# Decoder block on one core: the router's logits, the scatter waits and one exponential put in other places

## The chip, the cores and the metric

One core of one Trainium2 chip runs the whole kernel in one launch. The metric is the device time of that launch in microseconds, lower is better. In what follows PE is TensorE, DVE is VectorE, ACT is ScalarE, POOL is GpSimd, SP is SyncE.

## What is computed

A decoder block on x of shape (16, 256, 256): 16 sequences of 256 tokens of width 256, 16 heads of 16. All in float32.

```python
x = _layernorm(x + self_attention(x))       # causal; q and k normalised per head before the scores
x = _layernorm(x + cross_attention(x, ctx)) # rotary q and k, no mask, biases
x = _layernorm(x + moe(x))                  # 8 experts, 2 per token

def moe(x):
    logits = x @ router_w.T                 # (tokens, 8)
    top_logits, top_idx = top_k(logits, 2)
    probs = softmax(top_logits)
    hmid = gelu(x @ w1[e].T + b1[e]); y = hmid @ w2[e].T + b2[e]
    return sum over the two experts of probs * y
```

## The kernel before

**Blocks and quarters.** The attention part is a software pipeline over 32 blocks: n = 0 to 15 is the self attention of sequence n, n = 16 to 31 ("crossed") the cross attention of sequence n - 16. A block has four head groups, and the pipeline advances by quarters: `for q in range(QUARTERS)`, 153 of them, with r = q % 4. Every engine has this loop written out by hand, and calls in each quarter the steps that are due: `block_at(q, AT)` gives the block n for which q = 4n + AT, `group_at(q, AT)` the block and head group for which q - AT is their running number. Scores are at 8 (so they run in q = 8 to 135), exponentials at 13, the weighing of the values at 14. PE makes the scores twice: once (L531 to L538) for the row maxima that DVE takes (L1158), and once transposed (L561) with the maxima laid in, for ACT's exponential (L904); then it weighs the values (L582), and ACT drains that (L915). PE's scores of a quarter also wait for the exponential of the transposed scores of the quarter before, since they share banks.

**What else a quarter holds.** r = 0: first query and key projection (L635, qk0), transposes of the finished rows (L608, drained by ACT at L880 into x2T), the maxima's transpose. r = 1: second projection (L635, qk1), transposes of the queries (L669, qT, drained at L955), and the router's logits (L718, `rate`), four matmuls of x2T with 8 columns. r = 2: the output's transposes (L680, jobs o0 and o1; DVE divides them at L1252 and L1256), the value projection, the keys' transposes. r = 3: transposes of the divided output (L694, drained by ACT at L890 into onT), output projection (L706, wo), DVE's residual (L1268), and for a batch the counting of tokens per expert (L731, L734). For crossed blocks DVE drains qk0 and qk1 itself, in the rotation (L1225 to L1227). The logits belong to blocks 16 to 31, in q = 89 to 149; a second projection stands in the same quarter in the first ten of them (q = 89 to 125).

**The ring.** All these PE jobs but the scores share two PSUM banks. `ring_places()` walks the quarters in PE's order and numbers the jobs; a job's bank is its number modulo 2, and it waits until the job two numbers before has been drained:

```python
def await_room(pe, job):
    if RING[job] >= 2:
        pe.wait_ge(drained_by(job), RING[job] // 2)
```

In an r = 1 quarter of the crossed part the ring's order is pv, qk1, qT, logits, so the logits wait for the drain of qk1, which is DVE's rotation.

**The router.** DVE copies the logits (L1289, `take_logits`), here at the start of the following r = 2 quarter, and for batches of blocks, mostly two (four tiles of 128 tokens), chooses the first expert (`choose_first`, L1297 to L1305) and the second (`choose_second`, L1319 to L1327, with the same steps in `best`). For a batch that ends in block `last` the first choice is in q = 4 last + 28, the second in q = 4 last + 29; for the last three batches both are in q = 4 last + 26. Every step of a choice waits for the one before it. ACT makes one exponential of the difference of the two logits (L1000, `exp_gap`), in r = 3, after waiting for the second choice, and ahead of the drain of onT. DVE uses it in the same quarter (`combine_weights`, L1335 to L1351). One r = 0 quarter after, the places are known (L1380), and POOL scatters the rows, 128 at a time, into `xs_dram` by indirect transfers (L1615), two in each quarter from then on, each pair behind a wait for the scores of quarter q. Batches end in blocks 17, 19, 21, 23, 25, 27, 29, 30 and 31; those up to 25 have their first pair in q = 4 last + 32. POOL also adds the bias to each block's residual input in r = 0, ahead of that quarter's scatters (L1586, `add_bias`, for block n in q = 4n + 16); it needs the rows and the projection of block n - 2.

**After the quarters** the expert stage runs over 71 tiles (L813 to L835 on PE), and then the last normalisation.

Of the kernel before, what the change touches and what calls it, by code (L numbers as in the profile page):

```python
# [50 lines left out]
LOGITS_AT = 25  # L51
# [32 lines left out]
def ring_places():  # L84
# [7 lines left out]
    for q in range(QUARTERS):  # L92
# [8 lines left out]
        if r == 0:  # L101
            place("qk0", block_at(q, QK_AT))
            n = block_at(q, LN_AT)
            place("x2T", n, n is not None and crossed(n))
        elif r == 1:
            place("qk1", block_at(q, QK_AT + 1))
            place("qT", block_at(q, TURN_Q))
            n = block_at(q, LOGITS_AT)
            place("logits", n, n is not None and crossed(n))
        elif r == 2:  # L110
            place("o1", block_at(q, OUT_AT))
            place("v", block_at(q, V_AT))
            place("kT", block_at(q, TURN_K))
        else:
            n = block_at(q, TURN_X1)
            place("x1T", n, n is not None and crossed(n))
            place("wo", block_at(q, PROJECT_AT))
            place("rank", routed_at(q, RANK_AT))
# [6 lines left out]
def decoder_block(nc, x, xT, ctxT, wqk_self, wv_self, wo_self, wq_x, wk_x, wv_x, wo_x, bo_self, bo_x,  # L125
# [4 lines left out]
    with ExitStack() as ctx:  # L130
# [366 lines left out]
        def _(pe):  # L497
# [265 lines left out]
            for q in range(QUARTERS):  # L763
# [14 lines left out]
                if r == 0:  # L778
                    project_qk(block_at(q, QK_AT), 0)
                    turn_x2(block_at(q, LN_AT))  # L780
                elif r == 1:
                    project_qk(block_at(q, QK_AT + 1), 1)
                    turn_qk("qT", block_at(q, TURN_Q), 0)
                    rate(block_at(q, LOGITS_AT))
                elif r == 2:
# [63 lines left out]
        def _(act):  # L849
# [152 lines left out]
            for q in range(QUARTERS):  # L1002
# [6 lines left out]
                elif r == 3:  # L1009
                    seed_roots(block_at(q, CHAIN_AT), block_at(q, ROOT_AT))  # L1010
                    exp_gap(routed_at(q, RANK_AT))
                    drain_onT(block_at(q, PROJECT_AT))
# [12 lines left out]
                else:  # L1025
                    drain_x1T(block_at(q, TURN_X1))

            act.wait_ge(table_ready, 2)
# [45 lines left out]
        def _(dve):  # L1074
# [307 lines left out]
            for q in range(QUARTERS):  # L1382
# [9 lines left out]
                elif r == 1:  # L1392
                    maxima(group_at(q, SCORE_AT), 0)
                    maxima(group_at(q, SCORE_AT), 1)
                    moments_of(block_at(q, MOMENTS_AT))
                    choose_second(routed_at(q, SECOND_AT))
                    rotate(block_at(q, QK_AT + 1), 1)
                elif r == 2:
                    take_logits(block_at(q, LOGITS_AT + 1))
                    maxima(group_at(q, SCORE_AT), 0)  # L1400
# [142 lines left out]
        def _(pool):  # L1543
# [54 lines left out]
            def scatter(q):  # L1598
                for last in BATCHES:
# [9 lines left out]
                    ends = nt * TOPK if q == QUARTERS - 1 else min(2 * j + 2, nt * TOPK)  # L1609
                    u = group_at(q, SCORE_AT)  # L1610
                    if u is not None:
# [103 lines left out]
```

## Time and profile before

| | |
|---|---|
| median of 3 runs | 1186.8 us (1186.4 to 1188.1) |
| the profiled execution's own time | 1184.3 us |
| its span | 1182.6 us |
| mean granted clock of TensorE | 0.952 |
| PE busy | 1033.5 us (87%) |
| DVE busy | 720.5 us (61%) |
| ACT busy | 597.2 us (51%) |
| POOL busy | 268.0 us (23%) |

Busy time is the union of an engine's instructions over the span. The timeline gives for each instruction (or run of like ones) its start in microseconds from the span's start, its length, and in brackets how long the engine had stood idle and what released it. `x2` means two instructions in one row; for PE the count is of passes recorded. "issue" as a releaser means that the profile shows none close to the start. The granted clock is a share of full speed: 1.00 is 2.4 GHz, 0.50 is 1.2 GHz.

### The profile page before, as it was taken

To read this page: it belongs to the slowest core of one execution; us is meant where nothing else is said; L and a number is where in the kernel's file an instruction comes from. 1 tells how busy PE (TensorE), PEld (TensorE's weight loads), DVE (VectorE), ACT (ScalarE), POOL (GpSimd) and SP (SyncE) were. 2 spreads that over 40 slices of the span, in tenths; PEclk is the share of its full clock that TensorE was granted. 3 is DMA by queue.
4 is the path that set the end of the run, shared out by engine and by line. 5 is a ranking of instruction groups with operands and counts; after the bars stand their busy time and mean duration, and the time that the engine had idled before them with its cause. 6 is when DMAs were issued, how large, how long until landed. Compare 5 with 4: busy or idle time off the path is not lost.

```text
span 1182.6 us, 29067 instructions
## 1 busy us (share of the span) xinstructions
PE 1033.5 (87%) x10925; PEld 769.5 (65%) x10925; DVE 720.5 (61%) x1584; ACT 597.2 (51%) x1024; POOL 268.0 (23%) x309
## 2 busy tenths in 40 slices
PE   6899999999999999998999999876379999999930
PEld 3556666666666666666666666544269999999930
DVE  4656666666677777676768777763524444444446
ACT  3567767767755666565555555644122222222225
POOL 1053332322233200001212111132512222222210
PEclk9999999999999999999999999998579999999975
DMA  7117446455440001000000100011167766777656
GB/s 286 29 41 252 136 162 199 133 180 182 132 134 20 20 12 46 11 11 30 30 30 30 36 23 30 12 40 39 68 199 216 215 215 215 216 216 213 204 198 250
DMA packets 95078, 139.25 MB, mean 118 GB/s; under 512 B 11264, under 2 KB 68992, under 8 KB 93920
## 3 DMA queue, kind: packets, MB, share of 16 engines
q1 hardware_dynamic: 88320, 114.98, 31.2%
q0 software_dynamic: 6624, 22.42, 4.9%
q8 instruction: 91, 1.49, 0.5%
q14 instruction: 43, 0.35, 0.1%
HBM read 76.56 MB, written 60.29 MB: 116 GB/s over the span
## 4 chain that ended last, share of the span: by engine, by line
PE 80%; issue 6%; DVE 6%; ACT 4%; DMA 3%; SPq 1%; another core or an unknown queue 0%; ACTq 0%; DVEq 0%; POOLq 0%
PE PS L824 11%; PE PS L561 11%; PE PS L835 10%; PE PS L582 10%; PE PS L531 5%; PE PS L639 5%; PE PS L635 5%; PE PS L706 4%; PE PS L653 4%; PE PS L680 3%; PE PS L538 2%; PE PS L669 2%; ACT pT L904 2%; PE PS L534 2%; DVE part L1158 1%
## 5 line engine op out<-in xcount | busy, mean ns | idle before, releaser
L1158 DVE TENSOR_REDUCE part<-PS 128x6 f32<-128x768 f32 (+1 forms) x256 | 269.9, 1087 | 126.9 <-PE PS L538 84.8
L904 ACT ACTIVATE pT<-PS 128x768 f32<-128x768 f32 (+1 forms) x256 | 220.9, 915 | 94.1 <-PE PS L561 92.1
L561 PE MATMUL PS<-big 32*128 32x256 f32 (+1 forms) x2048 | 133.5, 373 | 21.3 <-issue 13.7
L1595 POOL TENSOR_SCALAR_AFFINE_SELECT pT<-pT 128x512 f32<-128x512 f32 x128 | 84.5, 661 | 279.0 <-ACT pT L904 275.4
L824 PEld LDWEIGHTS PS<-oT,big 128*128 128x128 f32 x1136 | 139.5, 194 | 5.4 <-ACT oT L1034 1.8
L824 PE MATMUL PS<-oT,big 128*128 128x128 f32 x1136 | 140.2, 277 | 1.0 <-ACT oT L1034 1.0
L561 PEld LDWEIGHTS PS<-big 32*128 32x128 f32 x2048 | 96.2, 185 | 64.3 <-issue 62.9
L582 PE MATMUL PS<-pT,vaug 128*32 128x256 f32 (+1 forms) x2048 | 126.3, 364 | 10.4 <-DVE carry L1365 2.3
L835 PE MATMUL PS<-w2s,qkn 128*128 x568 | 134.5, 380 | 0.2 <-issue 0.2
L1034 ACT ACTIVATE oT<-PS 128x256 f32<-128x256 f32 x71 | 27.3, 384 | 191.9 <-PE PS L813 191.9
L915 ACT ACTIVATE oT<-PS 128x256 f32<-128x256 f32 x128 | 49.1, 384 | 143.9 <-PE PS L582 125.0
L1615 POOL DMA_INDIRECT xs_dram<-rows_all,posi x64 | 62.2, 972 | 251.1 <-DVE posi L1380 185.3
L1636 POOL DMA_INDIRECT p_dram<-pT,rowid x71 | 68.9, 970 | 210.7 <-DVE rowid L1489 206.5
L835 PEld LDWEIGHTS PS<-w2s,qkn 128*128 128x128 f32 x568 | 102.4, 190 | 11.7 <-issue 0.7
L582 PEld LDWEIGHTS PS<-pT,vaug 128*32 128x32 f32 x2048 | 58.8, 110 | 62.5 <-issue 38.0
L1473 DVE TENSOR_TENSOR qkn<-PS,b1T 128x512 f32<-128x512 f32 x71 | 49.1, 692 | 60.8 <-PE PS L824 60.8
L1483 DVE TENSOR_TENSOR pT<-PS,w_self 128x256 f32<-128x256 f32 x71 | 30.1, 425 | 88.7 <-PE PS L835 88.7
L531 PE MATMUL PS<-big 32*128 32x256 f32 x1024 | 74.4, 404 | 4.4 <-ACT pT L904 4.4
L639 PE MATMUL PS<-w_self,xin 128*128 128x512 f32 x128 | 66.5, 645 | 2.7 <-DMA xin<-xT 1.4
L531 PEld LDWEIGHTS PS<-big 32*128 32x128 f32 x1024 | 47.1, 185 | 16.7 <-issue 14.3
L1041 ACT ACTIVATE qkn<-qkn 128x512 f32<-128x512 f32 x71 | 44.7, 630 | 19.7 <-DVE qkn L1473 18.8
L1586 POOL TENSOR_TENSOR xb<-rows_all,bo 128x512 f32<-128x512 f32 x16 | 20.5, 1280 | 127.8 <-DVE y L1268 125.3
(170 smaller groups left out, 1535.9 us busy)
## 6 DMA issues: line engine op xcount, KB each, us to landing
big<-w SPq DMA_DIRECT2D x71, 512.0 KB
xs_dram<-zrow SPq DMA_DIRECT2D x24, 1496.0 KB, 9.2
oT<-xs_dram SPq DMA_DIRECT2D x71, 136.0 KB
xin<-xT SPq DMA_DIRECT2D x16, 256.0 KB, 2.9
w2s<-w POOLq DMA_DIRECT2D x1, 4096.0 KB, 16.4
xb<-x SPq DMA_DIRECT2D x16, 256.0 KB, 11.2
xin<-ctxT SPq DMA_DIRECT2D x16, 256.0 KB, 2.8
big<-nmaxT SPq DMA_DIRECT2D x128, 4.0 KB
```

The lines of the kernel that those rows point to most:

```text
L531: ins = pe.matmul(o, q, a[r0:r1, 1, g, :], start=True, stop=True)
L561: ins = pe.matmul(o, keys, a[r0:r1, 0, g, q0:T], start=True, stop=True)
L582: ins = pe.matmul(o[PADDED * i:PADDED * (i + 1), q0:T], vaug[:, n % 4, kt, head(g, i), :], pT[:, k % 2, i, kt * T:kt * T + T - q0], start= ...
L635: ins = pe.matmul(o[:, e0:e0 + E], a1[:, c, t * P:(t + 1) * P], w[:, c, :], start=(c == 0), stop=(c == KC - 1))
L639: ins = pe.matmul(o, a[:, c, t * P:(t + 1) * P], w_qk[:, c, :], start=(c == 0), stop=(c == KC - 1))
L824: ins = pe.matmul(moe_bank(1, j % 2)[:, f * P:(f + 1) * P], w1s[:, j % W1_BUFFERS, c, f * P:(f + 1) * P], xsT[:, j % 2, c * P:(c + 1) * P] ...
L835: ins = pe.matmul(moe_bank(3, j % 2)[:, 0:E], hact[:, j % 2, c * P:(c + 1) * P], w, start=(c == 0), stop=(c == FC - 1))
L904: act.activation(pT[:, k % 2, 2 * half:2 * half + 2, 0:wide], src, ACT.Exp).then_inc((exp_a, exp_b)[half], 1)
L1158: dve.tensor_reduce(dst, src, AX.X, ALU.max, negate=True).then_inc((max_a, max_b)[half], 1)
L1595: pool.affine_select(d, d, [[0, 2], [0, 2], [1, P]], ALU.is_ge, 0.0, base=0, channel_multiplier=-1).then_inc(masked, 1)
L1615: pool.indirect_dma_start(out=xs_dram, out_offset=bass.IndirectOffsetOnAxis(ap=posi[:, batch_index(last), c:c + 1], axis=0), in_=rows_all[ ...
L1636: pool.indirect_dma_start(out=p_dram, out_offset=bass.IndirectOffsetOnAxis(ap=rowid[:, o, 0:1], axis=0), in_=ye[:, o], in_offset=None).the ...
```

## The change

Three things. The logits (`rate`) go to the front of the other r = 1 jobs on PE, in the ring and in the code, and DVE's copy of them goes ahead of the rotation in the same quarter. POOL's pairs of scatters wait for the scores of quarter q + 1 instead of q. ACT's `exp_gap` goes from ahead of the drain of onT to the end of the r = 3 quarter.

```diff
@@ ring_places
         elif r == 1:
+            n = block_at(q, LOGITS_AT)
+            place("logits", n, n is not None and crossed(n))
             place("qk1", block_at(q, QK_AT + 1))
             place("qT", block_at(q, TURN_Q))
-            n = block_at(q, LOGITS_AT)
-            place("logits", n, n is not None and crossed(n))
@@ TensorE
                 elif r == 1:
+                    rate(block_at(q, LOGITS_AT))
                     project_qk(block_at(q, QK_AT + 1), 1)
                     turn_qk("qT", block_at(q, TURN_Q), 0)
-                    rate(block_at(q, LOGITS_AT))
@@ ScalarE
                     seed_roots(block_at(q, CHAIN_AT), block_at(q, ROOT_AT))
-                    exp_gap(routed_at(q, RANK_AT))
                     drain_onT(block_at(q, PROJECT_AT))
...
                 else:
                     drain_x1T(block_at(q, TURN_X1))
+                    exp_gap(routed_at(q, RANK_AT))
@@ VectorE
                     choose_second(routed_at(q, SECOND_AT))
+                    take_logits(block_at(q, LOGITS_AT))
                     rotate(block_at(q, QK_AT + 1), 1)
                 elif r == 2:
-                    take_logits(block_at(q, LOGITS_AT + 1))
                     maxima(group_at(q, SCORE_AT), 0)
@@ GpSimd, scatter(q)
-                    u = group_at(q, SCORE_AT)
+                    u = group_at(q + 1, SCORE_AT)
                     if u is not None:
                         pool.wait_ge(scores_pe, NG * u[0] + u[1] + 1)
```

On PE, in the r = 1 quarter of a crossed block with a second projection (L582 weighing, L561 transposed scores, L635 projection, L669 queries turned, L718 logits, then L531 and L680 of the next quarter); a piece of the difference, the same in all ten:

```order
 L582 MATMUL PS<-pT,vaug 32x256 x8
 L561 MATMUL PS<-big 128x256 x8
-L635 MATMUL PS<-wx_q,x1T 128x256 x2
-L635 MATMUL PS<-wx_k,xin 128x256 x2
-L669 MATMUL PS<-ident,qkn 128x128 x4
 L718 MATMUL PS<-rw,x2T 128x8 x4
+L635 MATMUL PS<-wx_q,x1T 128x256 x2
+L635 MATMUL PS<-wx_k,xin 128x256 x2
+L669 MATMUL PS<-ident,qkn 128x128 x4
 L531 MATMUL PS<-big 128x256 x8
 L680 MATMUL PS<-ident,oT 128x128 x4
```

The logits went from the last place of the quarter to the one behind the transposed scores; nothing else moved on PE.

On ACT, in q = 143 and after, where the last block's output is drained (L890) and batch 29 has its exponential (L1000). Before:

```order
L982 ACTIVATE chain<-vv,eps 128x2
L984 ACTIVATE chain<-chain 128x2
L1000 ACTIVATE odds<-odds 128x4
L890 ACTIVATE onT<-PS 128x512
L991 ACTIVATE rows_all<-y,shift,chain 128x256 x2
```

And now:

```order
L982 ACTIVATE chain<-vv,eps 128x2
L984 ACTIVATE chain<-chain 128x2
L890 ACTIVATE onT<-PS 128x512
L1000 ACTIVATE odds<-odds 128x4
L991 ACTIVATE rows_all<-y,shift,chain 128x256 x2
```

The drain and the exponential changed places; the normalising of the rows stays behind both.

On POOL nothing changes its place, only the number that the waits on `scores_pe` name. In the changed kernel, from the last pair of batch 17 to the first of batch 19 (L1586 is the addition of the bias):

```order
L1615 DMA xs_dram<-rows_all,posi 34816x272 [waits scores_pe]
L1615 DMA xs_dram<-rows_all,posi 34816x272
L1586 TENSOR_TENSOR xb<-rows_all,bo 128x512 [waits ring_drained_0,row_ready] x2
L1615 DMA xs_dram<-rows_all,posi 34816x272 [waits scores_pe,place_ready,cw_ready]
L1615 DMA xs_dram<-rows_all,posi 34816x272
```

Two additions (blocks 22 and 23) stand directly behind the last pair, as they do before the change.

## Rows read from the trace of the kernel before

**Rows 1.** Page, parts 1 and 4: engine's busy time; the chain that ended last
```profile
PE 1033.5 (87%) x10925; PEld 769.5 (65%) x10925; DVE 720.5 (61%) x1584; ACT 597.2 (51%) x1024; POOL 268.0 (23%) x309
...
PE 80%; issue 6%; DVE 6%; ACT 4%; DMA 3%; SPq 1%; another core or an unknown queue 0%; ACTq 0%; DVEq 0%; POOLq 0%
```

**Rows 2.** Waits of PE, 470 to 780 us: total, times, longest
```profile
PE PS L718 <- DVE sq L1227: 14.1, 10, 1.8
```

**Rows 3.** Timeline, q = 105: start, length, engine, line, operation [idle before]
```profile
580.93 0.60 ACT L880 ACTIVATE x2T<-PS 128x512 f32<-128x512 f32 x1 [0.40 <-PE PS L608]
...
586.27 0.60 PE L669 MATMUL PS<-ident,qkn 128*128 128x128 f32 x4
...
587.11 0.16 DVE L1327 TENSOR_TENSOR odds<-top 128x4 f32<-128x4 f32 x1
...
588.68 1.03 PE L718 MATMUL PS<-rw,x2T 128*128 128x8 f32 x8 [1.81 <-DVE sq L1227]
```

**Rows 4.** Windows (core busy PE, PEld, DVE, ACT, POOL; clock; DMA), then timeline
```profile
478.00:481.30 3.30, 3.30 (x28) 1.97 (x32) 1.46 (x3) 0.00 (x0) 0.00 (x0) 0.50 0.03 7
...
676.00:679.30 3.30, 3.30 (x28) 1.52 (x28) 2.90 (x4) 0.07 (x1) 1.92 (x2) 0.50 0.14 47
...
589.64 1.19 PE L531 MATMUL PS<-big 32*128 32x256 f32 x16
...
597.65 1.15 PE L531 MATMUL PS<-big 32*128 32x256 f32 x16
...
619.13 1.15 PE L531 MATMUL PS<-big 32*128 32x256 f32 x16
...
625.62 1.15 PE L531 MATMUL PS<-big 32*128 32x256 f32 x16
```

**Rows 5.** Timeline: transposed scores with and without scatters; a pair's first scatter
```profile
556.08 1.15 PE L561 MATMUL PS<-big 32*128 32x256 f32 x16 [0.51 <-issue]
...
583.37 1.15 PE L561 MATMUL PS<-big 32*128 32x256 f32 x16 [0.25 <-issue]
...
627.61 0.97 POOL L1615 DMA_INDIRECT xs_dram<-rows_all,posi  x1 [4.25 <-PE PS L531]
```

**Rows 6.** Timeline, q = 133 and the start of q = 134
```profile
776.44 1.15 PE L561 MATMUL PS<-big 32*128 32x256 f32 x16 [0.77 <-issue]
...
779.69 1.94 ACT L904 ACTIVATE pT<-PS 128x1024 f32<-128x1024 f32 x2 [1.91 <-remote]
...
780.86 1.26 PE L531 MATMUL PS<-big 32*128 32x256 f32 x16 [2.28 <-ACT pT L904]
```

**Rows 7.** Timeline, end of q = 103, q = 104: POOL, VectorE, scores
```profile
571.46 0.97 POOL L1615 DMA_INDIRECT xs_dram<-rows_all,posi  x1 [0.30 <-issue]
...
571.68 0.15 DVE L1177 SCALAR_TENSOR_TENSOR chain<-chain 128x2 f32<-128x2 f32 x1
...
571.87 1.90 DVE L1180 SCALAR_TENSOR_TENSOR chain<-vv,chain 128x2 f32<-128x2 f32 x1
...
572.46 1.28 POOL L1586 TENSOR_TENSOR xb<-rows_all,bo 128x512 f32<-128x512 f32 x1
...
574.85 1.15 PE L531 MATMUL PS<-big 32*128 32x256 f32 x16
...
578.54 0.19 DVE L1299 TENSOR_TENSOR sel<-lg,top 128x32 f32<-128x32 f32 x1
...
580.55 0.69 DVE L1225 TENSOR_TENSOR qkn<-PS,cs 128x512 f32<-128x512 f32 x1 [1.14 <-PE PS L635]
```

**Rows 8.** Timeline, q = 143: last output turn, exponential, drain, residual
```profile
824.21 1.08 PE L694 MATMUL PS<-ident,on 128*128 128x128 f32 x4 [2.25 <-issue]
...
826.82 0.20 ACT L1000 ACTIVATE odds<-odds 128x4 f32<-128x4 f32 x1 [7.63 <-issue]
...
826.93 0.58 ACT L890 ACTIVATE onT<-PS 128x512 f32<-128x512 f32 x1
...
831.38 0.69 DVE L1268 TENSOR_TENSOR y<-PS,xb 128x512 f32<-128x512 f32 x1 [3.94 <-PE PS L706]
```

## Prediction

> **What bounds the kernel now.** The page first: TensorE is busy 87% of the span and the chain that ended last is 80% PE [rows 1]. PE runs its instructions in program order, so in the crossing part of the program every idle stretch of PE is lost time, unless a later wait would have taken it anyway. I then asked who PE waits for between 470 and 780 us [rows 2]: the first line is the router's logits (L718), idle for 14.1 us over 10 quarters until the second rotation of VectorE (L1227) is done. Nothing else comes near.
>
> The timeline of one such quarter (q = 105) shows why [rows 3]. PE works without a gap of note up to the turning of the queries, which ends at 586.87. The logits are next in the ring, two jobs behind the second projection, so they need the bank that the rotation reads. VectorE is still choosing experts until 587.27 and rotates only then; PE stands for 1.81 us. The logits' own data lay ready long before: the copy x2T ended at 581.53. The choice falls into four of the ten quarters; the other six share the rest of the 14.1 us, 1.15 each.
>
> **The change, part by part.**
>
> *Logits first.* On PE the four logits matmuls move ahead of the second projection, on VectorE their copy moves ahead of the rotation. The logits now need only x2T and the bank of x2T, both free. No instruction is added. The wait removed is all of the 14.1 us. What could wait instead: the turning of the queries, two jobs behind the logits, needs the copy (0.17 us) that VectorE does after the choice. That makes 587.27 + 0.2 = 587.5; PE, with 1.03 us of logits put in ahead, is through the projection at about 587.35 (the turning started at 586.27). So 0.15 us in the four quarters with a choice, 0.6 in all. The rotation takes its 1.4 us and ends at about 588.9, while the next scores start at 588.1 and end at 589.25 (1.15 long), and the first output turn wants that bank after them: 0.3 us of margin. The drain of the turned queries ends near 589.6 and is wanted at 589.9. Both margins are thin; as I work it out they hold. Term: -13.5 us.
>
> *Clock.* After three of these waits the granted clock fell to its lower level (1.2 GHz, 0.50 in the window) for 3.4 us; the first and the last of the three stand in [rows 4]. The quarter with the second of them took 8.01 us (589.64 to 597.65) where one at 2.4 GHz took 6.49 (619.13 to 625.62): 1.5 us each. Before each fall PE had stood idle and then run the logits, 8 columns wide. Between -4.6 and 0 (or a little above, if new waits do the same); I take all three as gone, since the nearest rows with such a gap have both parts side by side, and only the logits stay. Term: -4.6 us.
>
> *Transfers.* POOL issues four pairs of row scatters for each batch. The wait is the same instruction in the same place; its value is that of the next quarter's scores. A pair starts 1.99 us after a quarter's scores start (627.61 [rows 5] against 625.62). So the first pair leaves the end of an r = 0 quarter, and the last goes from the r = 3 quarter to the next r = 0 quarter; the other quarters keep a pair at the same point. Three effects.
>  - Without the first pair the maxima of the next quarter start sooner: PE's gap before the transposed scores is 0.51 us there against 0.25 without scatters [rows 5]. Four quarters, 0.2 each: -0.8 us.
>  - At q = 133 four scatters run one behind the other, and the release of the exponential comes 2.1 us behind the end of the matmuls that it needs; PE stands 2.28 us for it at 780.86 [rows 6]. With two scatters I expect about half of it: -1.1 us (bounds -2.3 and 0).
>  - The pair's new place collides. Behind each last pair POOL runs two additions of the bias, which the excerpt of POOL's order shows back to back. The row on L1180 is the warning: this VectorE instruction, with two inputs in SBUF, takes 1.90 us where L1177, its like, took 0.15, and ends with POOL's addition at 573.74; it was held from 0.41 us after the second scatter began [rows 7]. In the r = 3 quarter nobody was waiting. In q = 104 the pair will start at 574.85 + 1.99 = 576.84, the second scatter at 578.11, the hold at 578.52: at 578.54 VectorE starts the choice's first comparison (L1299). That is held until about 580.4. The second addition then takes 1.28 us and holds the next one to about 581.8, and the remaining steps end near 582.4. The rotation, which started at 580.55, comes 1.35 to 1.95 us late; qk0's bank, the maxima and the transposed scores come late by as much, and PE has no slack there. I take 1.65 for q = 104, 112 and 120, and 1.1 for q = 128, where no rotation stands behind the choice: +6.0 us. Bounds: 0 (the choice slips through ahead of the additions) and 4 x 2.4 = +9.6.
>
> The Trainium skill, SBUF — State Buffer, "Who interferes with whom", says that a VectorE instruction with two SBUF inputs and a GpSimd instruction that reads SBUF exclude each other for the whole instruction, and that writing transfer descriptors needs the other interface. It speaks against this change's new place for the additions. Taken to the letter, the hold would begin only with the addition's record, at 579.1; nearly all of the choice would be done, and the sum would be about 6 us lower. The 1.90 us of L1180 began 0.59 us before that record, so I go by the row.
>
> *Exponential.* exp_gap moves from ahead of the drain of onT to the end of ScalarE's r = 3 quarter. In the early batches it takes 0.19 us and nobody waits on either side. At q = 143 it matters: PE had turned the last block's output by 824.21 + 1.08 = 825.29, but ScalarE stood in exp_gap's wait until VectorE's choice was through, ran it at 826.82, and only then drained onT (826.93); the output projection followed and the residual at 831.38 waited 3.94 us for it [rows 8]. Now onT can be drained at 825.35: 1.55 us earlier, and from the residual a single chain (moments, normalising, logits, choice, last scatters) runs to the end of the phase. In this chain exp_gap(30) and (31) have nothing behind them that they held. Bounds 0 and -1.6. Term: -1.55 us.
>
> The expert stage after 860 us and the final normalisation keep order and data: 0.
>
> **Sum:** -13.5 - 4.6 - 0.8 - 1.1 + 6.0 - 1.55 = -15.5 us. The profiled execution took 1184.3 us (span 1182.6), so it would be 1168.8; the median of the runs is 1186.8, 2.5 above it, and I put the forecast on the median: **1171.3 us**.
>
> **The rivals.**
>  - *A, no collision.* The choice's comparisons get in ahead of the additions. For it: L1177, with the same kind of inputs, ran through at 571.68 in 0.15 us while the scatter was being issued. Against it: L1180, 0.2 us later, did not. -15.5 - 6.0 = -21.5: 1165.3 us.
>  - *B, the clock falls as often as before.* The new waits of about 1.7 us in the q = 105 kind of quarter come shortly before the logits, and the clock's lower stretches stay three. For it: seven of ten waits made no fall, so it is partly chance. -15.5 + 4.6: 1175.9 us. The Trainium skill, TensorE: Matmul & The Clock Gate, "HAM oscillation", says that gaps in TensorE's work bring the lower clock and that closing them keeps it up; by that the three stretches go, and the trace agrees only so far as each of them stands right behind a gap.
>  - *C, the wait moves on.* The thin margins of the next quarter (0.3 us for the first output turn and for the drained queries) are not there, because semaphores near scatters come late [rows 6]: with 0.8 us in each of ten quarters PE gets 8 us less. -15.5 + 8: 1179.3 us. For it: in a quarter with a choice VectorE goes from the choice into the copy and the rotation without a pause. Against: six of the ten quarters have no choice, and the rotation follows the projection at once.
>  - *D, slower.* The pair with its two additions occupies POOL for 4.9 us just where VectorE has 1.1 us of slack (idle before L1225) and ScalarE 0.4. If the late release (2.1 us), the hold (1.9) and the second addition (1.3) add up in series instead of overlapping, and a lower clock (1.5) follows each, a batch costs 6.8 us; four cost 27.2 instead of 6.0, and -15.5 + 21.2 = +5.7: 1192.5 us. It decides from 5.4 us a batch, the gains of 21.5 shared by four. Against it: the three run at the same time in the rows, and their overlap is almost whole.
>  - *E, no effect of the logits' move.* If the ring's next wait took all of it, only the smaller terms would be left, within 0.2% of before. That is the measurement's own uncertainty, 2.4 us.
>
> **How the numbers follow.** The forecast 0.42, A 0.20, B 0.16, C 0.13, D 0.04, E 0.05. The range reaches from just below A to most of the way to C: 1164 to 1178.5. By itself the forecast's case has 1168 to 1174 (the collision between 1.35 and 1.95 us, the q = 133 term between its bounds). Faster by over 0.2%: forecast, A, B, C, 0.91. Within 0.2%: E, 0.05. Slower: D, 0.04.
>
> **What would show it.** Right: L718 no longer has a VectorE release in PE's waits; an r = 1 quarter with projection takes about 7.0 us instead of 8.2 to 8.8; few lower-clock stretches between 470 and 780 us; L1180 is short everywhere, while an L1299 or L1301 in q = 104, 112, 120 lasts over 1 us, and the weighing or the transposed scores of the following quarter wait for VectorE; the residual of the last block comes 1.5 us after the choice's end less than before, at about 3 us behind it. Wrong: PE waits of 0.5 us or more before L680 in r = 2 quarters (C); no long L1299 or L1301 (A); a wait of 3 us or more in q = 105 (D).

## The result, and the profile after

| | before | changed |
|---|---|---|
| median, measured side by side | 1187.45 us (1186.4 to 1191.03, 4 runs) | 1169.41 us (1169.01 to 1171.78, 4 runs) |
| ratio | | 0.9847, 95% interval 0.9822 to 0.9872 |
| profiled execution | 1184.3 us | 1169.3 us |
| its span | 1182.6 us | 1167.6 us |
| mean granted clock | 0.952 | 0.956 |

The change is faster by 18.0 us in the medians and by 15.0 us in the spans of the two profiled executions. The forecast was 1171.3 us, from a sum of -15.5 between profiled executions. One run of e8 took 1258.13 us at a granted clock of 0.824, where its others have 0.954 to 0.957; its ratio below leaves that run out, its median doesn't (1163.54 us without it). The page of the changed kernel, parts 1 and 4, against [rows 1]:

```profile
PE 1029.7 (88%) x10925; PEld 767.3 (66%) x10925; DVE 724.1 (62%) x1584; ACT 596.7 (51%) x1024; POOL 267.0 (23%) x309
...
PE 80%; issue 6%; DVE 5%; ACT 3%; DMA 2%; SPq 2%; another core or an unknown queue 0%; ACTq 0%; DVEq 0%; POOLq 0%
```

PE bounds it as before. DVE is the one engine that is busy for longer (3.6 us more). PE's waits between 455 and 770 us (total, times, longest), against [rows 2]:

```profile
PE PS L531 <- ACT pT L904: 5.2, 6, 2.3
PE PS L582 <- DVE sq L1227: 3.5, 3, 1.2
PE PS L561 <- issue: 2.4, 8, 0.4
PE PS L582 <- ACT big L955: 2.3, 5, 0.5
PE PS L582 <- DVE carry L1365: 2.3, 5, 0.9
...
PE PS L669 <- DVE lg L1289: 0.7, 4, 0.2
```

The 14.1 us before the logits are gone. In their place stand four waits of 0.17 us for the copy of the logits (four of 0.15 were forecast), and two that take something back: the weighing waits for the rotation (3.5 us in three quarters), and the scores wait for the exponential (5.2 us; before, the same view has it at 0.9 us). Most of both comes from the quarters to which the last pair of scatters has moved, as q = 104 with the start of q = 105. The timeline of the changed kernel, all engines:

```profile
569.36 0.97 POOL L1615 DMA_INDIRECT xs_dram<-rows_all,posi  x1 [4.34 <-PE PS L531]
...
570.63 0.97 POOL L1615 DMA_INDIRECT xs_dram<-rows_all,posi  x1 [0.31 <-ACT oT L915]
...
571.06 3.12 DVE L1299 TENSOR_TENSOR sel<-lg,top 128x32 f32<-128x32 f32 x1
571.63 2.49 POOL L1586 TENSOR_TENSOR xb<-rows_all,bo 128x512 f32<-128x512 f32 x2
...
572.98 1.94 ACT L904 ACTIVATE pT<-PS 128x1024 f32<-128x1024 f32 x2 [2.64 <-remote]
...
574.14 1.15 PE L531 MATMUL PS<-big 32*128 32x256 f32 x16 [0.73 <-ACT pT L904]
...
576.38 1.07 PE L582 MATMUL PS<-pT,vaug 128*32 128x256 f32 x16 [1.09 <-DVE sq L1227]
```

L1299 normally takes 0.19 us [rows 7]. Here it starts at 571.06, 0.57 us before the record of the two additions, and ends at 574.18, with the end of the second (571.63 + 2.49 = 574.12). PE then waits twice, 0.73 us before the scores for an exponential that started late and 1.09 us before the weighing for the rotation: 1.8 us together. L1299 is held in the same way in q = 112, 120 and 128 (3.13, 3.13 and 3.10 us). In the last of these no rotation follows, and nothing on PE waits for VectorE. There the exponential starts 1.71 us behind the end of its matmuls (734.54, beside the two scatters), PE waits 2.29 us for it, and the clock falls (0.50 from 737.50 to 740.90):

```profile
737.42 2.06 PE L531 MATMUL PS<-big 32*128 32x256 f32 x16 [2.29 <-ACT pT L904]
```

A second new wait stands in q = 136, where batch 25 has its four scatters in a row:

```profile
775.74 0.39 PE L561 MATMUL PS<-big 32*128 32x256 f32 x4
...
778.62 1.94 ACT L904 ACTIVATE pT<-PS 128x1024 f32<-128x1024 f32 x2 [2.60 <-remote]
...
780.70 1.15 PE L561 MATMUL PS<-big 32*128 32x256 f32 x16 [2.42 <-ACT pT L904]
```

The matmuls that the exponential needs ended at 776.13; it started 2.5 us later (a late release, in what follows). q + 1 = 136 has no scores, so the last pair of this batch has no wait any more and runs right behind the pair before it. The wait stood there before too, at 0.99 us. Behind the longer one the clock falls a second time (a granted clock of 0.53 from 781.70 to 785.10). The timeline at q = 143, against [rows 8]:

```profile
811.38 1.09 PE L694 MATMUL PS<-ident,on 128*128 128x128 f32 x4 [2.27 <-DVE on L1256]
...
812.50 0.60 ACT L890 ACTIVATE onT<-PS 128x512 f32<-128x512 f32 x1 [6.18 <-issue]
...
813.15 3.39 PE L706 MATMUL PS<-wx_o,onT 128*128 128x256 f32 x8 [0.69 <-issue]
...
816.58 0.69 DVE L1268 TENSOR_TENSOR y<-PS,xb 128x512 f32<-128x512 f32 x1 [1.99 <-PE PS L706]
```

ScalarE drains onT 0.03 us after PE's end, where it stood 1.6 us before.

Where the 15 us went, by the start of each quarter's scores in the two timelines (changed less before): -0.6 lay before the first quarter that the change touches; the ten r = 1 quarters with a second projection, their new waits taken off, gave -14.5; three quarters behind a fall of the clock (q = 90, 106, 118) -4.3; a new fall of the clock in q = 129 some +1.4; the new place of the last pair +5.7 over four batches; q = 133 and 134 -3.0; q = 136 and after +2.3, of which the longer wait makes 1.4 and the second new fall 0.8; the last block -1.95; all other quarters +0.2. That makes -14.8, and the last block's residual stands at 816.58 against 831.38, 14.8 us earlier. The 18.0 us between the medians are more than these two traces account for.

### The profile page after: what moved, and what is told of

Read it like the earlier page. It is cut to its first block, busy times and chain, and to the rows that moved or that the text cites. A ratio compares the mean times of both kernels' runs of the same rounds, so it can differ in the third digit from the quotient of the medians.

```text
span 1167.6 us, 29067 instructions
## 1 busy us (share of the span) xinstructions
PE 1029.7 (88%) x10925; PEld 767.3 (66%) x10925; DVE 724.1 (62%) x1584; ACT 596.7 (51%) x1024; POOL 267.0 (23%) x309
## 4 chain that ended last, share of the span: by engine, by line
PE 80%; issue 6%; DVE 5%; ACT 3%; DMA 2%; SPq 2%; another core or an unknown queue 0%; ACTq 0%; DVEq 0%; POOLq 0%
PE PS L824 11%; PE PS L561 11%; PE PS L835 11%; PE PS L582 10%; PE PS L531 5%; PE PS L635 5%; PE PS L639 5%; PE PS L706 5%; PE PS L653 4%; PE PS L680 3%; PE PS L538 2%; PE PS L669 2%; PE PS L534 2%; ACT pT L904 2%; PE PS L813 1%
## 5 line engine op out<-in xcount | busy, mean ns | idle before, releaser
L561 PE MATMUL PS<-big 32*128 32x256 f32 (+1 forms) x2048 | 133.2, 373 | 20.4 <-issue 11.7
L561 PEld LDWEIGHTS PS<-big 32*128 32x128 f32 x2048 | 95.9, 184 | 62.5 <-issue 61.2
L582 PE MATMUL PS<-pT,vaug 128*32 128x256 f32 (+1 forms) x2048 | 125.0, 361 | 13.6 <-DVE sq L1227 3.5
L582 PEld LDWEIGHTS PS<-pT,vaug 128*32 128x32 f32 x2048 | 58.8, 109 | 64.7 <-issue 39.5
L531 PE MATMUL PS<-big 32*128 32x256 f32 x1024 | 74.2, 404 | 7.0 <-ACT pT L904 6.8
L531 PEld LDWEIGHTS PS<-big 32*128 32x128 f32 x1024 | 47.4, 186 | 20.8 <-issue 18.9
L1268 DVE TENSOR_TENSOR y<-PS,xb 128x512 f32<-128x512 f32 x32 | 22.1, 692 | 40.9 <-PE PS L706 37.3
```

What stands on the lines that cost most here:

```text
L531: ins = pe.matmul(o, q, a[r0:r1, 1, g, :], start=True, stop=True)
L561: ins = pe.matmul(o, keys, a[r0:r1, 0, g, q0:T], start=True, stop=True)
L582: ins = pe.matmul(o[PADDED * i:PADDED * (i + 1), q0:T], vaug[:, n % 4, kt, head(g, i), :], pT[:, k % 2, i, kt * T:kt * T + T - q0], start= ...
```

## Experiments

They were measured in sets: e1 to e4, e5 to e8, e9 and e10, e11 and e12, each set with the kernel before in it. Between sets the absolute times differ: in the last two the kernel before had a median of 1173 and 1178 us, in the earlier ones of 1187 to 1191. It isn't the chip alone: e1 to e4 (1188.75 us before) and e9 and e10 (1173.32) ran on the chip with the same number. So only ratios, or two kernels of one set, are set against each other. "The change" means the whole of it.

**e1_logits: the logits' move alone.** The hunks of the diff on the ring, on TensorE and on VectorE; scatter waits and exponential as before.

> The first part alone: the logits ahead of the second projection, in the ring, on PE and on DVE; the scatters wait as before and exp_gap stands as before. Theory (each part pays or costs what the comparison of the two traces says): the ten r = 1 quarters of q = 89 to 125 lose 1.15 to 1.8 us each and add 0.17 in the four with a choice, 13.5 us in all; the lower-clock stretches behind them go, 4.4 us; the last pair of scatters stays in the r = 3 quarter, so no L1299 lasts over 1 us and q = 104, 112, 120, 128 are as short as before; q = 133 still has its four scatters in a row and its wait of about 2.3 us. Ratio to before 0.984 to 0.986, about as fast as the whole change or 1 to 3 us faster. Rival (the scatter waits are part of the gain, and without them the late signals behind four scatters in a row now reach PE in q = 101, 109, 117, 125, where the stall on the rotation covered them before): PE waits of 1 us or more before the scores of q = 102, 110, 118, 126, and 4 to 8 us less gain, ratio 0.989 to 0.991.

Measured: 1168.22 us, ratio 0.983 (0.9799 to 0.9861). PE's waits, 455 to 770 us:

```profile
PE PS L531 <- ACT pT L904: 4.8, 5, 2.2
PE PS L561 <- issue: 4.3, 12, 0.7
PE PS L582 <- DVE carry L1365: 2.3, 5, 0.9
PE PS L582 <- ACT big L955: 2.0, 5, 0.5
```

No L718, and no L582 behind L1227. q = 104 takes 5.98 us and q = 105 7.22, against 6.78 and 8.02 in the change. The ten r = 1 quarters are 14.0 us shorter than before (13.5 were forecast), and the windows from 455 to 740 us all show a granted clock of 1.00. The scores of q = 135 start 18.5 us earlier than before (18.1 were in my two terms, logits and clock). The logits' move alone brings all that the change brings; nothing here shows that the other parts together add to it.

**e2_waits: the scatter waits alone.**

```diff
-                    u = group_at(q, SCORE_AT)
+                    u = group_at(q + 1, SCORE_AT)
```

> The second part alone: pairs of scatters wait for the next quarter's scores, everything else as before. Theory: L1299 lasts about 3.1 us in q = 104, 112, 120, 128, and each of these costs PE 1.6 us or more (q = 128 about 2.6), q = 136 with four scatters in a row costs about 2.2; q = 101, 109, 117, 125 give 0.2 each, q = 133 gives 2 to 3. Slower by 3 to 6 us, ratio 1.003 to 1.005. Rival (spreading the scatters pays by itself): faster by 1 us or more, ratio under 0.999.

Measured: 1196.06 us, ratio 1.0045 (1.002 to 1.007), slower by 5.4 us (2.4 to 8.3). PE's waits, 470 to 780 us:

```profile
PE PS L718 <- DVE sq L1227: 13.4, 10, 1.8
PE PS L531 <- ACT pT L904: 4.1, 6, 2.4
PE PS L582 <- DVE sq L1227: 4.1, 3, 1.5
```

The wait of the weighing for the rotation stands here too, 4.1 us in three quarters: it comes from the scatter waits, not from the logits' move. The three terms on transfers made +4.1 us. So this part of the change costs time. The trace shows one thing more. With the same ten waits for L1227 as before, five of the quarters behind them take 8.0 to 8.1 us and not 6.5 (q = 94, 102, 106, 114, 126), where it was three in the trace before; in that of e3 it is four (q = 90, 98, 110, 122). How often such a wait brings the lower clock differs from one execution to the next.

**e3_exp: the exponential alone.**

```diff
-                    exp_gap(routed_at(q, RANK_AT))
                     drain_onT(block_at(q, PROJECT_AT))
...
                     drain_x1T(block_at(q, TURN_X1))
+                    exp_gap(routed_at(q, RANK_AT))
```

> The third part alone: exp_gap behind the drain in r = 3. Theory: the residual of the last block comes 1.5 us earlier behind the choice (before: 4.6 us behind the start of L1327) and nothing else moves; 1.2 to 2 us faster, ratio 0.9984 to 0.9990. Rival (the chain behind the residual waits for something else, the scatters of batch 29 and 30 for one, or the exponential's later place costs combine_weights as much): within 0.5 us of before.

Measured: 1189.54 us, ratio 0.9994 (0.9972 to 1.0017). The time can't tell 1.5 us from nothing. The timeline at the last block can:

```profile
831.42 0.60 ACT L890 ACTIVATE onT<-PS 128x512 f32<-128x512 f32 x1 [6.01 <-issue]
...
832.86 0.21 ACT L1000 ACTIVATE odds<-odds 128x4 f32<-128x4 f32 x1 [0.85 <-issue]
...
835.89 0.69 DVE L1268 TENSOR_TENSOR y<-PS,xb 128x512 f32<-128x512 f32 x1 [2.40 <-PE PS L706]
```

The residual starts 3.03 us behind the exponential; before it was 831.38 - 826.82 = 4.56 [rows 8]. The local gain is 1.53 us at the same lower clock. That it reaches the end of the program is not shown by this run's time.

**e4_logits_exp: the change without the scatter waits.** The diffs of e1 and e3 together.

> First and third part, without the second. Theory: 13.5 + 4.4 + 1.6 = 19.5 us faster than before, ratio 0.983 to 0.985, and 1 to 5 us faster than the whole change, since the second part costs more in q = 104, 112, 120, 128 and 136 (1.6 x 3 + 2.6 + 2.2 = 9.6) than it gives in q = 101, 109, 117, 125 and 133 (about 3.8). Rival: the second part pays, and this is 2 us or more slower than the whole change.

Measured: 1166.22 us, ratio 0.9806 (0.9775 to 0.9837), against 0.983 for e1, measured beside it. From q = 101 to the end of q = 129 its trace gains 7.0 us on the change's, and loses 4.0 again in q = 133 and 134, where it still has four scatters in a row (7.18 and 7.75 us against 4.91 and 6.00). Its expert stage starts 3.0 us earlier. The ratios of this kernel and the change, from different sets, overlap at their ends; with e2 beside them, the scatter waits cost time where the additions stay in their place.

**e5_add_first: the additions of a crossed block ahead of the last pair, in place of behind it.**

```diff
-                if r == 0:
-                    add_bias(block_at(q, MAXT_AT + 4))
+                n = block_at(q, MAXT_AT + 4)
+                if n is not None and not crossed(n):
+                    add_bias(n)
...
+                n = block_at(q, MAXT_AT - 1)
+                if n is not None and crossed(n):
+                    add_bias(n)
```

> The whole change, and POOL's additions of the bias for crossed blocks put into q = 4n + 11 behind the masks, so ahead of the last pair of scatters instead of behind it; they need the residual of block n - 2, which is made in that quarter. Theory (the 3.1 us of L1299 are the two additions, and they cost PE its wait before the weighing in q = 105, 113, 121 and part of q = 128): every L1299 is back at 0.19 us, PE's wait on L1227 before L582 (1.09 to 1.19 us, three times) is gone, PE's wait of 0.7 us for the exponential at the end of q = 104, 112, 120 stays or grows a little, since that one belongs to the scatters. 2.5 to 4.5 us faster than the whole change, ratio to before 0.981 to 0.9835. Rival (the scatters themselves hold DVE): L1299 or its neighbours stay above 1 us, and the time is that of the whole change within 1 us.

Measured: 1174.58 us, ratio 0.9869 (0.9844 to 0.9894); I had expected better than the change. L1299 is back at 0.19 us, and q = 105, 113 and 121 are 0.8 to 0.9 us shorter. But q = 100, 108, 116, 124 and 132 are 0.85 us longer each. PE's waits, 455 to 770 us:

```profile
PE PS L582 <- DVE carry L1365: 6.6, 5, 1.7
```

PE waited 2.3 us for L1365 in the change. Half of the additions now land in the quarters in which DVE counts the places (L1365). The hold went to other instructions of the same kind. Up to q = 135 gains and losses cancel. Behind it PE waits 4.16 us for the exponential before the transposed scores of q = 137, where the change waits 1.36, and e5 loses another 2.8 us up to the last output turn. There ScalarE's drain of the weighing starts 2.4 us behind its end (781.11, 783.50), beside two scatters and not four.

**e6_keep_135: e5, with the last pair of batch 25 waiting for the scores of q = 135.**

```diff
-                    u = group_at(q + 1, SCORE_AT)
+                    u = group_at(q + 1, SCORE_AT) or group_at(q, SCORE_AT)
```

> As the kernel with the additions first, and the last pair of batch 25 in q = 135 keeps a wait for the scores of q = 135 (the last there are), which the change had dropped. Theory (the drop let four scatters run in a row in q = 135, and that made PE wait 2.42 us for the exponential of q = 136): this wait on scores 135 is the one that the pair before already has, so the four still run in a row and nothing changes: within 1 us of the kernel with the additions first, PE wait of about 2.4 us before L561 in q = 136. Rival: the wait itself spaced them in the kernel before, and restoring it gives 2 us.

Measured: 1174.58 us, ratio 0.9861 (0.9836 to 0.9885), the same as e5, as expected. The reason was not quite the expected one: the wait of 2.4 us in q = 136 is 0.96 us in both, and in both 4.16 us stand in q = 137. Nothing is won by a wait for scores that have already started.

**e7_short_rows: fewer bytes in a scatter.** e4, with the scatters of batches 17 to 25 writing only the last 64 bytes of a row to a side tensor, and the whole rows written in one go after the quarters, so that its own time (one run, 1218.42 us) isn't to be compared.

```diff
+                            out=xs_side if early else xs_dram,
...
+                            in_=rows_all[:, t0 + c // TOPK, COL_CW if early else 0:ROW], in_offset=None
```

> First and third part, with the scatters of batches 17 to 25 sent during the attention as rows of 16 elements (64 bytes) into a tensor of their own, at the same points and with the same waits; the whole rows follow behind the last quarter, so the span is about 50 us longer and only q = 97 to 135 are read. Theory (the signals of PE come late because of the issuing of the transfers, 0.97 us each on POOL, not because of the bytes they move): ACT's exponential of q = 133 still comes 2 us behind the end of the transposed scores, and PE waits 2 us or more before the scores of q = 134, as in the kernel with whole rows. Rival (bytes): with 17 times fewer bytes the wait is under 1 us.

The timeline of e4 at q = 133, with whole rows, PE and ScalarE:

```profile
757.60 1.15 PE L561 MATMUL PS<-big 32*128 32x256 f32 x16 [0.75 <-issue]
...
760.72 1.94 ACT L904 ACTIVATE pT<-PS 128x1024 f32<-128x1024 f32 x2 [1.84 <-remote]
...
761.89 2.09 PE L531 MATMUL PS<-big 32*128 32x256 f32 x16 [2.16 <-ACT pT L904]
```

And in e7 (two source lines lower), with POOL's four scatters:

```profile
757.11 0.99 POOL L1618 DMA_INDIRECT xs_side<-rows_all,posi  x1 [25.40 <-DVE posi L1382]
758.41 0.96 POOL L1618 DMA_INDIRECT xs_side<-rows_all,posi  x1 [0.31 <-PE PS L533]
759.68 0.96 POOL L1618 DMA_INDIRECT xs_side<-rows_all,posi  x1 [0.30 <-issue]
760.94 0.97 POOL L1618 DMA_INDIRECT xs_side<-rows_all,posi  x1 [0.30 <-issue]
...
762.85 1.94 ACT L906 ACTIVATE pT<-PS 128x1024 f32<-128x1024 f32 x2 [1.87 <-remote]
```

In e4 the matmuls ended at 758.75 and the exponential started 1.97 us later; PE waited 2.16 us for it, and 2.18 in e7. With 17 times fewer bytes a scatter takes the same 0.97 us on POOL and the release is as late, in this one execution. So the bytes don't set it. That it is the issuing on POOL is what is left, not shown by itself: the number of rows written is the same in both. The scores behind the wait take 2.09 us in e4, 1.15 elsewhere: the clock falls there too (0.50 from 761.8 to 765.2).

**e8_last_spread: e4, with the scatters of batch 25 alone spread.** Its first three pairs wait one quarter longer, the last waits for the first exponential of q = 136.

```diff
-                    u = group_at(q, SCORE_AT)
+                    u = group_at(q + (last == B + 9), SCORE_AT)
...
+                    elif last == B + 9 and group_at(q + 1, EXP_AT) is not None:
+                        u = group_at(q + 1, EXP_AT)
+                        pool.wait_ge(exp_a, NG * u[0] + u[1] + 1)
```

> First and third part; of the second only batch 25: its first three pairs wait for the next quarter's scores, its last for the first exponential of q = 136. The other batches scatter as before. Theory: q = 133 and 134 take 4.9 and 6.0 us as in the whole change instead of 7.2 and 7.7, with no four scatters in a row anywhere, and neither the collision of q = 104, 112, 120, 128 nor the wait of q = 136: 3 to 5 us faster than first and third part alone, 5 to 8 faster than the whole change, ratio to before 0.976 to 0.979. Rival (what is gained in q = 133 comes back as a wait behind the last pair in q = 136 and 137, where the choice for batch 27 runs): within 1 us of first and third part.

Measured: 1164.19 us, ratio 0.9769 (0.9741 to 0.9797), the best ratio of all. PE's scores of q = 134 and 135 in its timeline:

```profile
761.34 1.15 PE L531 MATMUL PS<-big 32*128 32x256 f32 x16 [0.24 <-issue]
...
767.32 1.15 PE L531 MATMUL PS<-big 32*128 32x256 f32 x16 [1.58 <-ACT pT L904]
```

q = 133 is 4.90 us long where e4 has 7.18, q = 134 5.98 against 7.75; with the wait the lower clock behind it is gone. Against e5 and e6, measured beside it, the intervals are clear of each other; against e4, from another set, they overlap.

**e9_add_apart: the change, with the additions of the crossed blocks one quarter later, behind a wait for that quarter's scores.**

```diff
...
+                n = block_at(q, MAXT_AT + 5)
+                if n is not None and crossed(n):
+                    u = group_at(q, SCORE_AT)
+                    if u is not None:
+                        pool.wait_ge(scores_pe, NG * u[0] + u[1] + 1)
+                    add_bias(n)
```

> The whole change, with each addition of the bias for a crossed block put into q = 4n + 17 behind a wait for that quarter's scores, where DVE takes the maxima (one input, from PSUM). Theory (of what the last pair costs in the whole change, 0.8 us a batch is DVE's hold behind the two additions and another 0.8 the late exponential beside the scatters): L1299 is 0.19 us everywhere; q = 105, 113, 121 take 7.2 us instead of 8.0 to 8.1, q = 128 and 129 together 1.5 to 2 us less; q = 104, 112, 120 stay at 6.7 to 6.8, with PE's wait of about 0.7 us for the exponential; nothing is lost elsewhere, unlike in the kernel with the additions first. 3.5 to 4.5 us faster than the whole change, ratio to before 0.981 to 0.983. Rival (the hold is of the scatters, or the additions find another two-input instruction of DVE wherever they stand): an instruction of DVE over 1 us between q = 104 and 130, and less than 1 us gained.

Measured: 1151.72 us, ratio 0.9813 (0.9786 to 0.984). L1299 takes 0.19 us between q = 96 and 130; q = 104 takes 5.97 us, q = 105 7.24 and q = 128 4.91. One L1299 is held further on, for 1.55 us, in q = 136, where no scores are left for the addition to wait for. The ratio is the expected one, but not for the expected reasons alone: q = 104 was to stay at 6.7 to 6.8 us.

**e10_both: e8 and the additions of e9.**

> First and third part, the scatters of batch 25 spread as in the kernel before this call, and the additions apart as above. Theory: L1180's 1.9 us in the r = 3 quarters had nobody waiting for it, so this gives at most 0.5 us over the kernel with batch 25 spread; ratio 0.976 to 0.979. Rival: the residual and the maxima behind L1180 had been late by it, and each r = 3 quarter with scatters gets 0.3 us or more back: 1.5 us or more.

Measured: 1150.66 us, ratio 0.9801 (0.9775 to 0.9827), not told apart from e9, measured beside it. In both traces no release beside a scatter was late, so that the spreading had nothing to remove. That left a doubt: e9's gain could have come from this alone. The last two kernels, measured side by side, settle it.

**e11_after_again (the changed kernel, unaltered) and e12_apart_again (e9, unaltered).**

> The whole change once more, unaltered, beside the kernel with the additions apart, since in the call before the kernel before took 1173 us and not 1187 to 1191, and in its two traces no signal of PE came late beside scatters. Theory of the additions: L1299 over 3 us in q = 104, 112, 120, 128 whatever the day, and the additions apart are 3 us or more faster in the same call. Theory of the signals: whether they come late beside scatters is a matter of the execution, not of the additions' place: in one call both kernels show it (q = 104 at 6.7 to 6.8 us) or neither does (q = 104 at 6.0). Rival: the additions' place caused both, so in one call this kernel shows late signals and the other shows none.

> The additions apart once more, beside the whole change in the same call. Theory: every L1299 between q = 96 and 130 at 0.19 us, q = 105, 113, 121 at 7.2 us, 3 to 5 us faster than the whole change of the same call; late signals as in that kernel. Rival: no late signals here while the other has them, and 7 us or more between the two.

Measured: 1160.85 us, ratio 0.9864 (0.9847 to 0.9882), and 1152.86 us, ratio 0.9798 (0.9781 to 0.9815). The additions' place is worth 8.0 us here, more than the 3 to 5 that I had expected. The rival's 7 us or more came out as a number but not as a mechanism: neither trace has late releases. Timeline of e11, q = 104 and 105 (DVE, PE), and q = 135 (ACT):

```profile
569.19 3.12 DVE L1299 TENSOR_TENSOR sel<-lg,top 128x32 f32<-128x32 f32 x1
...
571.48 1.15 PE L531 MATMUL PS<-big 32*128 32x256 f32 x16
574.52 1.60 PE L582 MATMUL PS<-pT,vaug 128*32 128x256 f32 x16 [1.90 <-DVE sq L1227]
576.05 2.09 PE L561 MATMUL PS<-big 32*128 32x256 f32 x16
...
773.19 1.94 ACT L904 ACTIVATE pT<-PS 128x1024 f32<-128x1024 f32 x2 [0.69 <-PE PS L561]
```

Windows of e11 (length, busy PE, PEld, DVE, ACT, POOL, then the granted clock):

```profile
560.00:590.00 30.00, 27.91 (x282) 18.96 (x278) 24.08 (x46) 17.24 (x30) 6.36 (x6) 0.94 0.12 38
...
680.00:710.00 30.00, 27.19 (x270) 18.71 (x269) 24.03 (x56) 16.22 (x27) 1.87 (x2) 0.94 0.02 5
```

Timeline and window of e12 at the same place:

```profile
570.70 0.97 POOL L1615 DMA_INDIRECT xs_dram<-rows_all,posi  x1 [0.30 <-ACT oT L915]
571.13 0.19 DVE L1299 TENSOR_TENSOR sel<-lg,top 128x32 f32<-128x32 f32 x1
...
574.63 1.07 PE L582 MATMUL PS<-pT,vaug 128*32 128x256 f32 x16
574.67 1.27 POOL L1586 TENSOR_TENSOR xb<-rows_all,bo 128x512 f32<-128x512 f32 x1 [3.01 <-PE PS L531]
...
560.00:590.00 30.00, 29.40 (x311) 20.29 (x309) 23.29 (x49) 19.38 (x32) 5.15 (x5) 1.00 0.12 39
```

No exponential is late in e11 (0.07 us behind its matmuls in q = 135, against 2.5 in the first trace), yet L1299 is held for the same 3.12 us. With nothing else late, PE waits for all of it at one point, 1.90 us, and behind that the clock falls in two of the four batches: the transposed scores take 2.09 us instead of 1.15. The quarters q = 105, 113, 121 and 129 are 2.7, 1.6, 2.8 and 1.3 us longer than in e12, 8.4 together. So in the first trace the 0.73 and 1.09 us were the same 1.8 us, cut in two. There q = 104 and 105 are together 1.6 us longer than in e4; the hold alone costs 1.6 in q = 113 of e11, and the late exponential alone 0.7 in q = 104 of e5. In those three batches it lay within the time that the hold would have cost anyway.

## Why the prediction was right, and where it was not

| term | forecast | the trace of the change |
|---|---|---|
| logits and first pair | -13.5 - 0.8 | -14.5 |
| clock | -4.6 | -4.3 + 1.4 |
| q = 133 and 134 | -1.1 | -3.0 |
| q = 136 and after | none | +2.3 |
| collision | +6.0 | +5.7 |
| exponential | -1.55 | -1.95 |

**Logits: right.** The wait went, the next one in the ring stood for 0.17 us in the four quarters named, and neither thin margin gave way: PE's wait for the queries' drain (L955) stayed at 2.3 us, before 2.1. e1 shows the term alone, at -14.0; what the first pair adds to it is 0.5 us (0.8 were forecast). Rivals C and E fall with it, and so does D: PE waits 1.09 us in q = 105, not 3.

**Clock: right for the three falls, others missed.** Two new falls come behind the two longest new gaps, 2.29 us in q = 129 and 2.42 us in q = 136, both waits for a late exponential. The step "I take all three as gone" left out that the scatters' new places make gaps of their own kind. Rival B, the clock falling as often as before, doesn't hold: between 455 and 790 us it falls four times before and twice in the change. That the term is three falls is the luck of one execution: with the same waits e2 has five and e3 four. e11 and e12 show the link with the hold: two falls with it, none between 560 and 770 us without it. The Trainium skill, TensorE: Matmul & The Clock Gate, "HAM oscillation", ties the lower clock to gaps; the traces agree so far as each new fall stands behind such a gap (2.29 and 2.42 us in the change, 1.90 in e11), while two others in e11, of 1.8 to 1.9 us, brought none.

**Collision: right place and size, wrong inside.** I let L1299 be held by the first addition for 1.9 us and the next step by the second. It was held through both, 3.12 us, so DVE was free at about the time I had worked out. With a single addition of 1.28 us behind it, in q = 136 of e12, it is held for 1.55 us. That it begins ahead of the addition's record was right (0.57 us; L1180 had 0.59): the rule in the Trainium skill, SBUF — State Buffer, "Who interferes with whom", taken to the letter with the times of the records, would have let most of the choice through, and the measurement decides against that reading. Whether the lock begins before the addition does, or the record of the addition begins late, the traces don't show. Rival A falls. L1180 is short again, 0.23 us at most. e5, e9 and e12 show that the additions hold it, and not the scatters: in e12 the two scatters run at the same place, L1299 starts 0.43 us into the second and takes 0.19 us. Behind q = 128 the change waits for the late exponential, which I had not priced at this place, and the hold lies within that wait; in e11, where nothing is late, the hold alone makes q = 129 longer by 1.3 us (1.1 were forecast).

**q = 133: mis-sized.** "With two scatters I expect about half of it" failed: the forecast took off 1.1 us, and 3.0 went. Two scatters left no late exponential there (PE's wait fell from 2.28 us to 0.23; in e8 to 0.24, from 2.16 in e4). That makes 2.4. The other 0.6, in q = 134, is a fourth fall of the clock, behind this wait in the kernel before, that I had not counted. Its window:

```profile
781.80:785.10 3.30, 3.30 (x28) 1.46 (x24) 2.84 (x4) 0.01 (x1) 1.85 (x2) 0.50 0.11 42
```

Two scatters aren't harmless as such: one quarter on, at q = 134, the change's exponential starts 1.0 us late beside two, and PE waits 1.60 us. What decides it stays open.

**q = 136: missed.** The step "a pair goes from the r = 3 quarter to the next r = 0 quarter" overlooked that for batch 25 no scores follow, so that the wait vanishes. The four scatters in a row, which had run in q = 133, now run up to q = 136 and took back 2.3 of the 3.0 us.

**Exponential: right.** 1.53 us in e3. In the change the output projection also ran at a higher clock (3.39 us against 3.78), which makes the rest.

The misses had opposite signs: in the table's order -0.2, +1.7, -1.9, +2.3, -0.3 and -0.4, 1.2 us together, and outside the terms -0.6 before the change begins and +0.2 elsewhere. So the sum came out 0.7 us off (-14.8 against -15.5; the rounded terms give 0.8). The large term, the logits, was right by its mechanism; that the rest came so close was luck. The sum hides what e1, e2 and e4 show: the scatter waits lose 5.4 us by themselves, and nothing shows that they pay in the whole.

**A version that beats both.** e4 and e8 beat the kernel before by 1.9 and 2.3% where the change does by 1.5 (e8's interval is clear of the change's, e4's overlaps it); e12, measured beside the change, beats it by 8.0 us. e8 was not measured beside e12 or e10 where scatters make releases late, so which of them is best there stays open. What differs between the sets with and without late releases stays open too.

## What to carry to other kernels

In a ring of shared banks, put the job whose inputs are ready ahead of the one that a slower engine drains: it cost one line per engine and was worth all of the gain. When transfers or small operations are moved on an idle engine, write down which instructions of the other engines they then stand beside, and test each moved part alone: here one part lost what another had won, and a sum that came out right didn't show it. For the last round of a loop ask what a wait on "the next quarter" means when there is none.

## What was not expected of the hardware

- A VectorE instruction of 0.19 us with two inputs in SBUF was held for 3.12 us, through two GpSimd additions back to back (1.27 us alone), with no gap between them to slip through. Its start was 0.57 us ahead of the additions' record. An indirect transfer being issued did not hold it (0.19 us).
- PE's results reached ScalarE 2.0 to 2.5 us late beside four indirect transfers being issued, as much with 64-byte rows as with whole ones, and up to 2.4 us late beside two; in the last two sets not at all with the same instructions in the same places (0.07 us). Nothing in the profiles says why.
- A gap of the same 1.8 to 1.9 us brought the lower clock in two batches of e11 and not in the other two. Ten waits of at most 1.8 us each brought it three, five and four times in the traces of three kernels that all have them.
